# Expert rows of three batches summed by GpSimd, and two first loads issued one stage earlier

## What is computed

```
# layer 0, end: each token's 8 expert rows (already weighted) are summed and added
x = x + jnp.tanh(g_ffn[0]) * _L0_ffn_ref(_layernorm(x), ...)
#   inside: out = (y_tok * w[:, None]).reshape(T, TOP_K, H).sum(axis=1)     TOP_K = 8, H = 256
# layer 1: a gated recurrent cell in its parallel form, then a block for half of the tokens
x = x + jnp.tanh(g_xattn[1]) * _L1_xattn_ref(_layernorm(x), ctx_1024, ctx_1024, ...)
x = x + jnp.tanh(g_ffn[1]) * _L1_ffn_ref(_layernorm(x), ...)
```

## Time and profile before

| | us |
|---|---|
| median of 3 runs | 2944.91 |
| lowest and highest of them | 2941.24, 2959.34 |
| the profiled execution, whole | 2945.35 |
| its span in the profile | 2943.6 |
| VectorE busy, of the span | 1828.4 (62%) |
| TensorE busy, of the span | 2481.0 (84%) |
| GpSimd busy, of the span | 755.3 (26%) |

### The profile page before, as it was taken

The page is one execution under the profiler, slowest core; times in us unless marked ns, Lnnn a source line. Parts: engine busy times, 40 slices in busy tenths (PEclk is TensorE's granted clock), DMA queues, the critical chain, the costliest instruction groups (busy, mean ns, idle before and its releaser), DMA issues. The chain is left out here.

```text
span 2943.6 us, 35609 instructions
## 1 busy us (share of the span) xinstructions
PE 2481.0 (84%) x12608; PEld 1335.9 (45%) x12608; DVE 1828.4 (62%) x4072; ACT 1170.7 (40%) x2095; POOL 755.3 (26%) x462
## 2 busy tenths in 40 slices
PE   6888972865888699889899979989988989997996
PEld 2333331323555344545554635554454545463554
DVE  5667745246867474477767357748437875835774
ACT  1433430212323153265544146635325653514662
POOL 1002352520000042043323023414203432402441
PEclk8999985875878799999999999999999999999998
DMA  7411006974200200244320124430023442012442
GB/s 226 136 37 21 11 15 206 316 249 150 87 8 3 106 1 1 87 108 119 97 79 8 73 61 118 116 111 11 8 88 100 116 108 79 1 52 71 110 125 73
DMA packets 112959, 257.06 MB, mean 87 GB/s; under 512 B 36198, under 2 KB 56294, under 8 KB 106762
## 3 DMA queue, kind: packets, MB, share of 16 engines
q1 hardware_dynamic: 93978, 220.26, 24.8%
q10 hardware_dynamic: 12656, 25.97, 3.6%
q0 software_dynamic: 6144, 8.48, 1.0%
HBM read 119.81 MB, written 29.69 MB: 51 GB/s over the span
## 5 line engine op out<-in xcount | busy, mean ns | idle before, releaser
L858 POOL TENSOR_SCALAR pbuf<-pbuf,recip 128x1024 f32<-128x1024 f32 x128 | 364.5, 2848 | 946.0 <-DVE recip L762 946.0
L807 ACT ACTIVATE pbuf<-ps,least 128x1024 f32<-128x1024 f32 x256 | 284.3, 1113 | 295.3 <-DVE least L755 219.5
L755 DVE CUSTOM_DVE_ANT_0 ps<-ps,mask 128x1024 f32<-128x1024 f32 x256 | 307.9, 1244 | 140.2 <-PE ps L687 139.2
L584 POOL TENSOR_SCALAR pbuf<-pbuf,recip 128x512 f32<-128x512 f32 x128 | 200.2, 1576 | 459.7 <-DVE recip L505 459.7
L687 PE MATMUL ps<-kH,qT 64*128 64x512 f32 x1024 | 267.4, 642 | 49.8 <-ACT pbuf L807 47.0
L712 PE MATMUL ps<-work,vh 128*64 128x256 f32 x2048 | 251.9, 390 | 0.0
L555 ACT ACTIVATE pbuf<-ps,least 128x512 f32<-128x512 f32 x256 | 172.7, 686 | 155.6 <-DVE least L495 155.6
L769 DVE STREAM_TRANSPOSE pbuf<-pbuf 128x2048 f32<-128x2048 f32 (+1 forms) x128 | 226.3, 1768 | 0.0
L1554 ACT ACTIVATE early<-ps 128x1536 f32<-128x1536 f32 x86 | 123.9, 1441 | 200.9 <-PE ps L1369 191.7
L1632 DVE TENSOR_REDUCE mh<-ps 128x3 f32<-128x1536 f32 x86 | 150.0, 1744 | 63.8 <-PE ps L1358 61.2
L712 PEld LDWEIGHTS ps<-work,vh 128*64 128x64 f32 x2048 | 138.3, 138 | 95.2 <-issue 36.6
(11 more groups left out here) (371 smaller groups left out, 4054.7 us busy)
## 6 DMA issues: line engine op xcount, KB each, us to landing
work<-pbuf SPq DMA_DIRECT2D x784, 96.0 KB, 2.5
work<-pbuf ACTq DMA_DIRECT2D x240, 96.0 KB, 2.9
early<-in_L_wgu SPq DMA_DIRECT2D x22, 768.0 KB
expert_rows<-zero_rows SPq DMA_DIRECT2D x16, 1024.0 KB, 11.5
yg<-expert_rows SPq DMA_DIRECT2D x16, 1024.0 KB, 6.0
early<-in_L_wd SPq DMA_DIRECT2D x22, 384.0 KB
arena<-in_L_wo SPq DMA_DIRECT2D x8, 1024.0 KB, 8.8
arena<-in_L_wff SPq DMA_DIRECT2D x4, 2048.0 KB, 9.3
```

The costliest lines, as they stand in the source:

```text
L584: nc.gpsimd.tensor_scalar(x, x, recip[:, n % 8:n % 8 + 1], None, mult).then_inc(probs_ready[1], 1)
L755: nc.vector.tensor_tensor_reduce(out=x, in0=x, in1=mask, scale=1.0, scalar=FMAX, op0=add, op1=ALU.min, accum_out=least[:, n % 8:n % 8 + 1])\
L807: nc.scalar.activation(to, x, ACT.Exp, bias=least[:, n % 8:n % 8 + 1], scale=-1.0, accum_out=sums[:, n % 8:n % 8 + 1]).then_inc(taken, 1)
L858: nc.gpsimd.tensor_scalar(unit(n), unit(n), recip[:, n % 8:n % 8 + 1], None, mult).then_inc(pool_divided, 1)
```

## The change

Four edits, all for the third stage.

1. The sums of tiles 4 to 15 (batches 1 to 3) are no longer in VectorE's list but in GpSimd's, in the same three steps with the same operands and a wait between the steps. VectorE keeps the four tiles of batch 0. `summed` becomes a pair of counters, one for each engine, and whoever waited for it waits for the engine in question. The first write of a batch to a `yacc` that an earlier batch used now waits for that batch's first layer norm (`xn_ready`).
2. The due numbers of the sums of batches 1 to 3 are lower.
3. The load of x of batch 0 and that of the transposed context of batch 0 are issued at the end of SP's list of the experts' stage, behind the last pair's weights, and count in semaphores that the third stage waits for. They are gone from the third stage.
4. The other batches' loads are as they were.

```diff
@@ experts, SP
                     load_pair(sp, a, places[n % WEIGHTS], n, came[n % WEIGHTS])
+                sp.dma_start(G["xb"][:, :, :], G["x_d"][0]).then_inc(G["x_first"], 16)
+                sp.dma_start(G["ctxT"][:, :, :], a["ctxT"][0]).then_inc(G["ctxT_first"], 16)
                 for i in range(RING):
@@ layer1
-    SUMS = ((-9, -6, -3, -0.5), (8, 13.5, 15, 32), (52, 62, 74, 84), (92, 99, 107, 122))
+    SUMS = ((-9, -6, -3, -0.5), (5, 10, 14, 18), (40, 46, 52, 57), (78, 84, 90, 96))
@@
+        x_in[0], ctxT_in[0] = G["x_first"], G["ctxT_first"]
@@ layer1, SP
                     if j >= YG:
-                        sp.wait_ge(summed, j - YG + 1)
+                        i = j - YG
+                        sp.wait_ge(summed[i >= NT], i + 1 if i < NT else i - NT + 1)
@@
-                x_load(0)
                 for j in range(NT):
                     rows(j)
                     if j == 0:
                         weights(early1)
-                    if j == 1:
-                        sp.dma_start(ctxTs[0][:, :, :], a["ctxT"][0]).then_inc(ctxT_in[0], 16)
@@ layer1, GpSimd
-                side_by_side(*chains(part))
+                add_link = Chain(pool, add_order)
+
+                def row_sums():
+                    for j in range(NT, TILES):
+                        b, t = divmod(j, NT)
+                        yield SUMS[b][t]
+                        y = yg[j % YG]
+                        pool.wait_ge(y_in[j % YG], 16 * (j // YG + 1))
+                        add_link(nc.gpsimd.tensor_tensor(y[:, 0:4, :], y[:, 0:4, :], y[:, 4:8, :], add))
+                        add_link(nc.gpsimd.tensor_tensor(y[:, 0:2, :], y[:, 0:2, :], y[:, 2:4, :], add))
+                        if t == 0 and b >= PAIR:
+                            pool.wait_ge(Ls[b % PAIR]["xn_ready"], 1)
+                        nc.gpsimd.tensor_tensor(yaccs[b % PAIR][:, t, :], y[:, 0, :], y[:, 1, :], add).then_inc(summed[1], 1)
+
+                side_by_side(row_sums(), *chains(part))
@@ layer1, VectorE
-                    v.wait_ge(summed, NT * (b + 1))
+                    v.wait_ge(summed[b > 0], NT * max(b, 1))
@@
-                    for j in range(TILES):
+                    for t in range(NT):
```

More of the change, by code:

```diff
@@ L979, in program @@
         gates_ready = sem("gates_ready")
+        x_first, ctxT_first = sem("x_first"), sem("ctxT_first")
         fill_ready = sem("fill_ready")
@@ L2176, in layer1 @@
         y_in = [sem(f"y_in_{i}") for i in range(YG)]
-        weights_in, small_in, summed = sem("weights1_in"), sem("small1_in"), sem("B_summed")
+        weights_in, small_in, summed = sem("weights1_in"), sem("small1_in"), [sem(f"B_summed_{n}") for n in "vp"]
+        add_order = sem("B_add_order")
         zero_ready, sum_order, gw_ready = sem("B_zero_ready"), sem("B_sum_order"), sem("B_gw_ready")
         x_in, ctxT_in, ctx_in = ([sem(f"B_{n}_in_{b}") for b in range(B)] for n in ("x", "ctxT", "ctx"))
+        x_in[0], ctxT_in[0] = G["x_first"], G["ctxT_first"]
         names = ("order", "xn_ready", "turned", "xnT_ready",
@@ L2679, in row_sums @@
                 def row_sums():
-                    for j in range(TILES):
[L2681 to L2684, removed]
+                    for t in range(NT):
+                        yield SUMS[0][t]
+                        y = yg[t % YG]
+                        v.wait_ge(y_in[t % YG], 16 * (t // YG + 1))
                         add_link(nc.vector.tensor_tensor(y[:, 0:4, :], y[:, 0:4, :], y[:, 4:8, :], add))
                         add_link(nc.vector.tensor_tensor(y[:, 0:2, :], y[:, 0:2, :], y[:, 2:4, :], add))
-                        nc.vector.tensor_tensor(yaccs[b % PAIR][:, t, :], y[:, 0, :], y[:, 1, :], add).then_inc(summed, 1)
+                        nc.vector.tensor_tensor(yaccs[0][:, t, :], y[:, 0, :], y[:, 1, :], add).then_inc(summed[0], 1)
                 side_by_side(row_sums(), *chains(part))
```

## The result

| | before | after |
|---|---|---|
| median, us | 2946.87 (13 runs) | 2963.94 (13 runs) |
| lowest and highest | 2941.24, 2959.97 | 2953.64, 2975.7 |
| span of the profiled execution | 2943.6 | 2962.2 |
| third stage, from SP's first issue to that of the next stage | 356.5 | 367.6 |

The ratio is 1.0048, with a 95% interval from 1.0030 to 1.0066: about 14 us slower (9 to 19). That is half a per cent, within the 1% that I had named as the bound; the median after is 15 us above the forecast.

What follows compares the result with a forecast made beforehand. No engine is full; a TensorE-ScalarE-VectorE chain bounds the stage, so sums cost time only where VectorE runs without pause. Terms: -2.4 - 2.35 - 2.3 - 3.45 + 7 + 7.0 = +3.5 us on 2945.35, giving 2948.9; range 2932 to 2962.

Steps and rivals of the forecast that it cites:

- A: Start of the third stage: two loads moved to the experts' stage let tile 3 land sooner, -2.4 us.
- B: Before batch 0's scan L2530: sums of tiles 5 and 6 leave VectorE, second half of the pair gained, -2.35 us.
- C: Tile 8's sum, at 728.13 in a VectorE run without pauses, leaves VectorE: -2.3 us.
- F: VectorE's run from 704.30 to 722.5: instructions wait while GpSimd reads for batch 2's sums, +7.0 us.
- E: Batch 0's Newton steps and scalings on VectorE, slowed by GpSimd's sums of batch 1: +7 us, bounds +2.3 and +14.
- D: Sums of tiles 10 to 14 leave VectorE's run from 768.00 to 811: -11.65 us of VectorE, at most -6.7 of time.
- G: VectorE's run from 768.00 to 792.7, slowed by GpSimd's batch 3 sums: +8.2 us; D + G = -3.45.
- the cap of 6.7: Limit on D's time gain: TensorE, close behind VectorE, allows at most 5.5 us by 799.76 and 1.2 more at 821.33.
- Rival 1: GpSimd and VectorE hardly disturb each other in the third stage: -8.5 us, 2936.9; chance 0.28.
- undisturbed case: No disturbance at all between GpSimd and VectorE in the third stage: -13.8 us, 2931.6; chance 0.04.
- Rival 2: Newton steps and scans crawl, one VectorE step for each GpSimd instruction: +17 us, 2962.4; chance 0.14.
- Rival 3: Moved loads gain nothing, landing late or tile 3 held by context packets: A = 0, +5.9 us, 2951.3; chance 0.06.

Runs made afterwards that it cites:

- the exchange: Changed kernel with GpSimd's two-input additions replaced by one-input multiplications of the same sizes; third stage 345.4 us, ratio 0.9976 to the kernel before.

## Why the prediction was right and where it was wrong

- **Right:** the change stays within 1%, and the time depends, as said, on what VectorE pays for GpSimd's additions. They cost 29.4 us (367.6 against 338.2), and the freed sums and moved loads give 18.3 back; forecast were 22.2 and 18.7. So the forecast of +3.5 was a third of the stage's 11.1. That it still fell within 1% owes as much to the width of that band, which held all rivals but one tail, as to the sum. No mask and no sum's consumer waited for the new work: batch 1's sums end at 671.35, the mask comes at 690; batch 2's begin right behind the fourth mask.
- **A, B, C** came out at -2.3, -2.3 and -2.2, **F** at +6.0 for 7.0. A tile costs GpSimd 4.45 us for 4.7.
- **E, +7, measured +12.7.** The step that failed is "eleven need two tiles of 4.7 instead of 2.2 us". The eleven small steps came 8.1 us later, 2 more than forecast: the block lasts for the whole two-input addition and not for 3.8 of 4.7 us. The one microsecond at L2524 did not come, since the sums had ended at 671.35, before L2522 began at 677.08. The other 4.5 us are the four scalings (5.92 for 1.38), which I had let run through as one block. They don't depend on each other, and still GpSimd gets in between each two of them. The bound of 14 held it.
- **D + G, -3.45, measured -0.75.** Both halves were wrong, in opposite directions. G is +11.0, near its upper bound of 13.2 and not 8.2, for the same reason as E. D is worth all of its 11.65 (11.8 without sums on GpSimd, 11.6 with them in pauses); the cap of 6.7 at TensorE was wrong as a step, although my sum did not use it. I had read TensorE's wait of 0.82 us as all that it could give, and had counted only the sums ahead of that wait. TensorE's next work hangs on VectorE's next piece, too, so its waits move with VectorE.
- **Rival 1** (hardly disturbed) is refuted; its undisturbed case, -13.8, was itself too small: 18.3 us are there. **Rival 2**, one VectorE step for each GpSimd instruction, is nearest: +17 forecast, E 12.7 and D + G -0.75 measured, 14 by the ratio. It had too small a chance. **Rival 3** (the loads gain nothing) did not occur in the changed kernel, and nearly did in others.
- The median after, 2963.94, lies 2 us above the range, which reached to 2962. The third stage alone, 11.1 us, would give 2956.5, which lies in it and just above the forecast's own range, 2943 to 2956.

## What to carry to other kernels

Two-input work moved from VectorE to GpSimd disturbed nothing where VectorE meanwhile neither read two SBUF tensors nor scaled one. Elsewhere price it as the rest of the GpSimd instruction for every such VectorE step that meets one, and count independent VectorE instructions one by one, since GpSimd gets in between them. A chain of small dependent steps is a bad neighbour (0.16 us becomes up to 2.26). Look first for the pauses of the engine that has the work: nine numbers in a table gave 0.65% here, where the second engine cost 0.5%.

## What was not expected of the hardware

- Two-input instructions of the two engines take turns. At 795 to 805 in the changed kernel VectorE's L116 (1.22 us) comes first and GpSimd's addition of 512 columns behind it lasts 2.33 instead of 1.27 us; VectorE's L117 behind that lasts 2.17, and four L2648 5.04 instead of 1.43:

```profile
795.60 1.22 DVE L116 TENSOR_TENSOR eT<-hb,mv 128x1024 f32<-128x1024 f32 x1
796.86 2.17 DVE L117 TENSOR_TENSOR eT<-eT,rstd 128x1024 f32<-128x1024 f32 x1
799.06 0.70 DVE L2645 TENSOR_SCALAR tmp<-vec,gates 128x256 f32<-128x256 f32 x1
799.79 5.04 DVE L2648 TENSOR_TENSOR eT<-eT,tmp 128x256 f32<-128x256 f32 x4
```

```profile
795.61 2.33 POOL L2288 TENSOR_TENSOR yg<-yg 128x512 f32<-128x512 f32 x1
```

- How long a GpSimd instruction blocks differs between its forms: 2.26 us of a two-input addition of 2.33, about 0.6 us at the start of a one-input multiplication of 1.53. GpSimd's busy time grew from 67.9 to 75.6 us by the exchange, and the stage still fell by 22 us.
- VectorE instructions with one of their inputs in PSUM (L2607, L2608 and L2572 at 722.55 to 723.49 in the changed kernel) ran in 0.34, 0.37 and 0.16 us, as before, beside GpSimd's additions of 721.65 and 723.05.
